# Scan: mix and scores as 64x64 quarters, keys of odd channel tiles with halves exchanged

## The reference, cut to what matters

```python
def step(state, inp):
    x_t, b_t, c_t, dt_t = inp
    decay = jnp.exp(dt_t * a)[..., None, None]
    b_bar = dt_t[..., None] * b_t
    state = decay * state + b_bar[..., None] * x_t[:, :, None, :]
    y_t = jnp.einsum('bhn,bhnp->bhp', c_t, state)
    return (state, y_t)
```

## Time and profile before

| | |
|---|---|
| median of 3 runs | 1251.53 us (1251.30 to 1253.37) |
| profiled execution | 1251.51 us, span 1249.4 us |
| PE busy | 1233.5 us, 99% of the span |
| PE weight load | 1029.7 us, 82% |
| DVE busy | 923.6 us, 74% |
| POOL busy | 775.0 us, 62% |
| ACT busy | 612.0 us, 49% |
| granted clock of PE | 1.000 |

### The profile page before, as it was taken

One profiled execution on the slowest core, in us unless ns is written; L12 is line 12 of the kernel. 1 busy time (PEld: TensorE's weight loads), 2 busy tenths in 40 slices (PEclk: granted clock), 3 DMA queues, 4 the chain that ended last, 5 costly groups with the idle time before them and its releaser, 6 DMA issues.

```text
span 1249.4 us, 28240 instructions
## 1 busy us (share of the span) xinstructions
PE 1233.5 (99%) x11183; PEld 1029.7 (82%) x11185; DVE 923.6 (74%) x1868; ACT 612.0 (49%) x1276; POOL 775.0 (62%) x660
## 2 busy tenths in 40 slices
PE   8999999999999999999999999999999999999999
PEld 4666678888888888888888887789989999899998
DVE  7999877777675677677766657897777766776676
ACT  6999974444434344433433334444344332554453
POOL 4889845345454476666766656566666754566773
PEclk9999999999999999999999999999999999999999
DMA  9799759353454444435434445574455544799995
GB/s 293 258 338 351 292 202 211 135 170 128 141 173 141 166 134 133 156 147 178 136 121 166 148 144 175 191 176 89 92 114 95 96 92 105 230 322 332 334 320 176
DMA packets 122211, 231.18 MB, mean 185 GB/s; under 512 B 19168, under 2 KB 85984, under 8 KB 113760
## 3 DMA queue, kind: packets, MB, share of 16 engines
q1 hardware_dynamic: 108928, 212.08, 50.5%
q0 software_dynamic: 12288, 17.05, 8.0%
q10 hardware_dynamic: 864, 0.24, 0.1%
HBM read 147.81 MB, written 81.53 MB: 184 GB/s over the span
## 4 chain that ended last, share of the span: by engine, by line
PE 76%; DVE 8%; ACT 4%; POOL 4%; DMA 3%; issue 3%; SPq 1%; POOLq 0%; another core or an unknown queue 0%; ACTq 0%; DVEq 0%
PE ps L1273 22%; PE ps L1613 9%; PE ps L1870 8%; PE ps L2104 7%; PE ps L2083 7%; PE ps L1398 4%; PE ps L1328 3%; PE ps L1410 2%; PE ps L1361 2%; PE ps L1378 2%; PE ps L1344 2%; DMA y_dram<-yb 2%; PE ps L693 2%; PE ps L641 1%; ACT decay L1240 1%
## 5 line engine op out<-in xcount | busy, mean ns | idle before, releaser
L1240 ACT ACTIVATE decay<-tap,ncum 128x128 f32<-128x128 f32 x344 | 105.4, 389 | 150.5 <-POOL tap L1153 150.5
L1798 POOL DMA_INDIRECT ffn_dram<-ob,idx x64 | 110.3, 1724 | 81.6 <-DVE ob L1717 67.8
L1071 DVE TENSOR_TENSOR yb<-ps,yb 128x256 f32<-128x256 f32 x128 | 48.4, 420 | 146.0 <-PE ps L1410 141.3
L1832 ACT ACTIVATE mid<-ps,b_up 128x512 f32<-128x512 f32 x96 | 65.9, 689 | 156.0 <-PE ps L1613 130.4
L1182 POOL TENSOR_SCALAR yb<-x,dcol 128x512 f32<-128x512 f32 x64 | 48.9, 764 | 129.9 <-DMA y_dram<-yb 95.3
L1159 POOL TENSOR_TENSOR x_lo<-x,x_hi 128x512 fp32r<-128x512 f32 x56 | 73.6, 1314 | 80.5 <-ACT x_hi L1226 80.4
L1170 POOL TENSOR_TENSOR c_dec<-cT,ecum_row 128x512 f32<-128x512 f32 x64 | 89.2, 1394 | 35.9 <-PE ps L1410 26.3
L1273 PE MATMUL ps<-x_hi,w_hi_b 128*128 128x512 f32 x240 | 99.6, 415 | 0.6 <-ACT bT L1230 0.6
L1273 PE MATMUL ps<-x_hi,w_hi_c 128*128 128x512 f32 x240 | 99.4, 414 | 0.0
L1959 POOL TENSOR_SCALAR yc<-yc,gn_scale,gn_shift 128x512 f32<-128x512 f32 x56 | 76.7, 1381 | 32.4 <-DMA yc<-y_dram 32.4
L1273 PE MATMUL ps<-x_lo,w_hi_b 128*128 128x512 f32 x240 | 94.4, 393 | 0.0
(11 more groups left out here) (313 smaller groups left out, 3948.0 us busy)
## 6 DMA issues: line engine op xcount, KB each, us to landing
tap<-cum_dram SPq DMA_DIRECT2D x43, 512.0 KB
x_dram<-x SPq DMA_DIRECT2D x16, 1024.0 KB, 5.7
x<-x_dram SPq DMA_DIRECT2D x16, 1024.0 KB, 5.6
ecum_row<-ecum_dram SPq DMA_DIRECT2D x128, 128.0 KB
y_dram<-yb SPq DMA_DIRECT2D x16, 1024.0 KB, 7.4
yc<-y_dram SPq DMA_DIRECT2D x16, 1024.0 KB, 6.8
cum_row<-cum_dram SPq DMA_DIRECT2D x21, 512.0 KB
rows_dram<-xn SPq DMA_DIRECT2D x16, 512.0 KB, 3.3
```

The source lines that it names most:

```text
L1240: n = nc.scalar.activation(decay[g % 2][:, h, :], cum_row[g % NR][:, h, :], ACT.Exp, bias=t.ncum[:, g, h:h + 1])
L1798: pool.indirect_dma_start(out=t.ffn_dram, out_offset=bass.IndirectOffsetOnAxis(ap=t.idx[:, e, h * HC + c:h * HC + c + 1], axis=0), in_=ob[ ...
```

## The change

The masked quarter is left out. The key halves are called p (where they lie: partitions 0 to 63 or 64 to 127). For queries of the first half only early keys count. So that both row halves of the PE array get equal work, the two key halves of odd channel tiles are exchanged: `key_half(q, p)` is p for even q and 1 - p for odd. Partition p of an odd tile then holds the other half of the chunk's tokens, in x2 (loaded in five DMAs, `load_turned`), in bT (ACT's copy), in dt, ncum, gap and the mask. Where the key half is the late one, scores and mix have 64 columns instead of 128. The mix contracts 64 keys at a time and sums the halves in two banks, ps_y[0] and ps_y[1], which are now full, so DVE adds two operations of 512 columns into yb. The update goes into ps_r (upper half), ahead of the mix in every chunk, and is started anew each time. The lists no longer accumulate in ps_r: each chunk's sum is added by DVE into SBUF (`add_lists`), and the two zero matmuls go. The store of y to memory is issued a chunk earlier (c == 0).

```diff
+def load_turned(sp, dst, src, loaded):
+    sp.dma_start(dst[:, 0:4:2, :], src[:, 0:4:2, :]).then_inc(loaded, 16)
+    for m in (1, 3):
+        for j in range(2):
+            sp.dma_start(halves(dst[:, m, :])[:, :, 1 - j, :], halves(src[:, m, :])[:, :, j, :]).then_inc(loaded, 16)
@@ front, DVE: gap, ncum and dt each as three operations
+            def do_turned(op, *aps, name):
+                parts = [a.rearrange("p t (a k i) -> p k t a i", a=2, k=2) for a in aps]
+                do(op(*(a[:, 0] for a in parts)))
+                for r in range(2):
+                    own, other = (slice(j * s.HD, (j + 1) * s.HD) for j in (r, 1 - r))
+                    do(op(parts[0][own, 1], *(a[other, 1] for a in parts[1:])), name if r else None)
@@ DVE, chunk(g)
+        def add_lists(k, g):
+            dve.wait_ge(tile_used, k + 1)
+            dve.wait_ge(s_mm, updates(g + 1))
+            flat = lists[:, :, :, :, :].rearrange("p a b k l -> p (a b k l)")
...
+                v.tensor_tensor(flat, ps_list, flat, ALU.add).then_inc(lists_read, 1)
-            for a in range(2):
-                own_half = yb[b % 2][:, 2 * a:2 * a + 2, cols]
-                n = v.tensor_tensor(own_half, ps_y[a][:, 0:HW].rearrange("p (m n) -> p m n", m=MT // 2), own_half,
-                                    ALU.add)
-            n.then_inc(y_ready, 1)
+            if LIST0 <= g < LIST1:
+                add_lists(g - LIST0, g)
+            y_out, (y_0, y_1) = yb[b % 2][:, :, cols], [a[:, :].rearrange("p (m n) -> p m n", m=MT) for a in ps_y]
+            v.tensor_tensor(y_out, y_0, y_out, ALU.add).then_inc(y_step, 1)
             update(g)
+            dve.wait_ge(y_step, g + 1 + g // SPAN + 1)
+            v.tensor_tensor(y_out, y_1, y_out, ALU.add).then_inc(y_ready, 1)
@@ SP
-            if c == 1 and b:
+            if c == 0 and b:
@@ POOL, causal(g)
+            nc.gpsimd.affine_select(out=even, in_=even, compare_op=ALU.is_ge, fill=-1e30, base=0,
+                                    pattern=[[0, H // 2], [1, P]], channel_multiplier=-1)
+            nc.gpsimd.affine_select(out=odd[:, :, 0:HD], in_=odd[:, :, 0:HD], compare_op=ALU.is_ge, fill=-1e30, base=HD,
+                                    pattern=[[0, H // 2], [1, HD]], channel_multiplier=-1).then_inc(row_ready, 1)
+            pool.wait_ge(row_ready, 2 * g + 1)
+            nc.gpsimd.affine_select(out=odd[0:HD], in_=odd[0:HD], compare_op=ALU.is_ge, fill=-1e30, base=-HD,
+                                    pattern=[[0, H // 2], [1, P]], channel_multiplier=-1).then_inc(row_ready, 1)
@@ PE, scores(g)
+                for p, a in ((0, 0), (1, 1), (1, 0), (0, 1)):
+                    n = (m + 2 * p) % MT
+                    r, j = slice(a * HD, (a + 1) * HD), key_half(n // 2, p)
+                    keys = bT[b % 2][r, n, c * P + p * HD:c * P + (p + 1) * HD]
+                    mm = pe.matmul(ps_g[a][p * HD:(p + 1) * HD, n * P + j * HD:(n + 1) * P],
+                                   keys, cT[b % 2][r, n, c * P + j * HD:(c + 1) * P],
@@ PE, update(g), ahead of the mix
+            pe.wait_ge(x_dt_ready, g + 1)
+            pe.wait_ge(b_w_ready, updates(g) + 1)
+            if g < ROUNDS:
+                pe.wait_ge(bit_step, 4 * g + 2)
+            elif SLOTS < g < SLOTS + CH:
+                pe.wait_ge(sel_step, steps[("limits", "offset", "slot_i")[g - SLOTS - 1]])
+            if g == LAST + 1:
+                pe.wait_ge(x.xg_lo_ready, 2 * s.KT)
+            elif g == LAST + 2:
+                pe.wait_ge(x.mid_ready, 2)
@@ PE, the mix
+            for r, tiles in enumerate(((0, 1), (2, 3), (1, 0), (3, 2))):
+                for i, p in ((0, 0), (1, 1), (1, 0), (0, 1)):
+                    q, rows = tiles[p], slice(p * HD, (p + 1) * HD)
+                    h, j = 2 * q + i, key_half(q, p)
+                    mm = pe.matmul(ps_y[p][i * HD:(i + 1) * HD, q * P + j * HD:(q + 1) * P],
+                                   x_dt[rows, h * HD:(h + 1) * HD], mix[rows, h, j * HD:P],
+                                   start=(r == 0), stop=(r >= 2), skip_group_check=True)
```

More of the change, by code:

```diff
@@ L535, in _ @@
                 tile_copy(n)
-            act.wait_ge(x2_back[1], 16)
+            act.wait_ge(x2_back[1], TURNED)
             for m in range(MT):
-                nc.scalar.activation(t.x_hi[1][:, m, :], x2[1][:, m, :], ACT.Copy).then_inc(x1_hi, 1)
+                nc.scalar.activation(*t.turned(t.x_hi[1][:, m, :], x2[1][:, m, :], m % 2), ACT.Copy).then_inc(x1_hi, 1)
             act.wait_ge(vec, steps["cum"])
@@ L908, in updates, with listed, added, key_half @@
         return g - g // SPAN
+    t.state_ready, t.updates = state_ready, updates
     def loads(b, n):
         return 16 * (b // n + 1)
+    def listed(g):
+        return min(max(g - LIST0, 0), LIST1 - LIST0)
+    def added(g):
+        bank = ps_pc if g == LAST + 1 else ps_pb if g == LAST + 2 else ps_r
+        return bank[:, LISTS:LISTS + MT * HD]
+    def key_half(q, p):
+        return p ^ (q % 2)
     @block.vector
@@ L1025, in update, with clear_y @@
                 dve.wait_ge(s_mm, updates(g) + 1)
-                v.tensor_tensor(state[:, :, :], added, state[:, :, :], ALU.add).then_inc(state_ready, 1)
+                v.tensor_tensor(state[:, :, :], new, state[:, :, :], ALU.add).then_inc(state_ready, 1)
+        def clear_y(g):
+            if g == 0:
+                dve.wait_ge(t.tile_out, 2 * MT)
+                for p in range(2):
+                    n = v.memset(ps_y[p][:, :], 0.0)
+            else:
+                dve.wait_ge(y_ready, g)
+                for p in range(2):
+                    q = 1 + p
+                    n = v.memset(ps_y[p][:, q * P:q * P + HD], 0.0)
+            n.then_inc(y_step, 1)
         def chunk(g):
@@ L1379, in _ @@
                 mm.then_inc(b_turned, 1)
+            until(pe, state_ready, updates(g))
             if g < ROUNDS:
                 total(g)
+            elif SLOTS <= g < SLOTS + CH:
+                slots(c)
             if b + 1 < NB:
@@ L1385, in _ @@
                 x.up(pe, 0, 0, range(2 * c - 2, 2 * c - 1))
+            until(pe, lists_read, listed(g))
             if LIST0 <= g < LIST1:
                 list_tiles(g - LIST0)
+            if not last:
+                update(g)
             until(pe, y_ready, g)
-            until(pe, state_ready, updates(g))
+            pe.wait_ge(y_step, g // SPAN * (SPAN + 1) + 1)
             pe.wait_ge(x_dt_ready, g + 1)
             pe.wait_ge(mix_ready, 2 * g + 2)
-            if first:
-                own_parts(g)
-            for a in range(2):
-                for m in range(MT):
-                    h = a * MT + m
-                    mm = pe.matmul(y_of(a, m), x_dt[:, h * HD:(h + 1) * HD], mix[:, h, :],
-                                   start=(m < 2 and not (first and a == 0)), stop=(first and m >= 2),
-                                   skip_group_check=True)
-            if first:
-                mm.then_inc(y_mm, 1)
-            elif not last:
-                own_parts(g)
+            mm = own_parts(g)
             if not first:
                 pe.wait_ge(c_dec_ready, g + 1)
-                for m in range(0, MT, 2):
-                    for i, a in ((0, 0), (1, 1), (1, 0), (0, 1)):
-                        r = slice(a * HD, (a + 1) * HD)
-                        mm = pe.matmul(y_of(a, m + i), state[r, m + i, :], c_dec[r, m + i, :], start=False,
-                                       stop=(m == MT - 2), skip_group_check=True)
-                mm.then_inc(y_mm, 1)
+                mm = state_parts(g)
+            mm.then_inc(y_mm, 1)
             if g + 1 < NT:
@@ L1609, in up @@
                 pe.wait_ge(mid_ready, n - 2)
+            if n in (0, 2, 4):
+                pe.wait_ge(t.state_ready, t.updates(s.NT - 3 + n // 2))
             i = 0
```

147 lines of the change are left out of this document (77 added, 70 removed).

## The result

The changed kernel takes 1246.01 us (median of 5, 1243.34 to 1251.24), the kernel before 1251.53; the ratio is 0.9944, 95% interval 0.9920 to 0.9967. So it is faster, but by 5.5 us where 16.0 were forecast, and 1246.0 against 1235.5.

The account below looks back on a forecast made before the run. PE was taken to bound the kernel, with DVE next. Terms: -26.0 (scores, mix) - 0.5 (lists' matmuls) + 6.5 (list stage) + 3.5 (end) + 0.5 (front) = -16.0, from 1251.53 to 1235.5 us; range 1229 to 1243.

Parts of the forecast that it names:

- Scores and mix, -26.0: Scores and mix on PE: masked quarters at 64 columns save 0.204 us each, 0.408 a chunk, 26.0 over 64 chunks.
- the 0.5 us of the lists' two matmuls: Lists on PE: dropping the 512-column matmuls that open and close the bank saves 0.5 us with their switches.
- The rival with 0.100 us a four: Scores and mix: four tiles don't go faster with fewer columns; fours gain only 4.6 us, about 1255 us; chance 0.07.
- The remark that the switches of form stay at one: PE array: the number of form switches stays; 128x64 to 64x64 moves from between update and state to update and mix.
- List stage, +6.5: 32 list chunks: DVE's longer loop makes PE wait for b_w; 5.8 us over 22 chunks, taken as 6.5 with POOL.
- one deadline, b_w before the update: List chunks: DVE's y-to-y loop through b_w takes 12.02 - i (i: wait before y); a chunk loses max(0, 2.74 - i).
- The mean of DVE's collisions: List stage: SBUF-only DVE operations stretch beside POOL; the second one-hot operation averages 1.12 us where b_w takes 0.68.
- End of the scan, +3.5: Chunks 61 to 63: update waits for token remainders (y 1.8 us later), DVE's additions and unsaved scores; sum 3.5 us.
- Costed at nothing: Stages without lists: b_w and y fit DVE's room; updates' waits in search and slot chunks are met before PE arrives.
- Hidden, as said: POOL's longer mask, x in five DMAs, halved mask-row loads and SP's extra DMAs: no cost in the scan.
- my bound of 12 us from the mean packet: Loads of x: each small piece at the queue's mean per packet, 93 ns, says 12 us more; hidden either way.
- The front, +0.5: Before chunk 0: split gap and ncum operations and later landing of x cost 0 to 4 us, taken as 0.5.

## Why the prediction was wrong, step by step

**Scores and mix, -26.0: right.** Full against short columns differ by 0.206 us for the scores and 0.206 for the mix (0.984 to 0.778, 0.924 to 0.718, medians of the list chunks), where the prediction had 0.204 each; PE's busy time fell by 25.2 (the 0.5 us of the lists' two matmuls can't be told apart in it). The rival with 0.100 us a four is out. The remark that the switches of form stay at one was right too, but I didn't see what hung on it: it holds only because the update went ahead of the mix, and the old order would have cost some 12 us, more than the change brings.

**List stage, +6.5: the step that failed.** It cost 9.4 us, and none of it by the way that the prediction took. I set DVE's loop against one deadline, b_w before the update. In the stage that wait doesn't occur once. DVE has an earlier one: x_dt before the turns of the keys, 5.2 us after the mix begins (587.66 and 592.85), with 0.77 us to spare. All that the change adds to DVE (0.34 for the lists, the second bank of y) stands ahead of it. Six chunks lost 5.9 us by it (five 1.02 to 1.04, one 0.74); the version with the addition moved gave back 4.1. The longer additions alone don't explain it, though: with the mix over 128 keys, where y is emptied in short ones, x_dt cost 6.0 us. What counts as much is where the decay starts among POOL's operations: with the list sum moved from ahead of it (and the second addition too) no decay was shut out for long. What POOL's mask in three operations has to do with it isn't shown. The mean of DVE's collisions was also wrong as a measure: its groups show

```profile
L1085 DVE TENSOR_TENSOR state<-state,dec 128x256 f32<-128x256 f32 x31 | 27.8, 896 | 0.0
L1050 DVE TENSOR_TENSOR spare<-chosen,cst 128x512 bf16<-128x512 f32 x30 | 22.7, 758 | 0.0
...
L1050 DVE TENSOR_TENSOR spare<-gateT,cst 128x512 bf16<-128x512 f32 x30 | 20.5, 684 | 0.0
...
L1064 DVE TENSOR_TENSOR lists<-ps,lists 128x256 f32<-128x256 f32 x31 | 13.2, 425 | 77.8 <-PE ps L1454 75.1 <-PE ps L1443 2.7
```

The one-hot operation `spare<-gateT` that took 1115 ns takes 684, so DVE collides less in sum, which is why b_w is early. But the decay went from 742 to 896, ahead of x_dt: a chunk has a collision of 1.7 us or none. The rest, 3.7 us in two chunks (periods of 11.21 and 10.76 for 9.29, with 0.3 in the next), is the stalls of PE without a releaser, which no part of the prediction had.

**End of the scan, +3.5: right in mechanism and nearly in size.** Chunks 60 to 63 lost 4.7. The update of chunk 61 waits 1.67 us for xg_lo (forecast 1.8):

```profile
775.49 1.29 DVE L1658 TENSOR_TENSOR xg_lo<-ps,xg_hi 128x512 fp32r<-128x512 f32 x2 [0.58 <-ACT xg_hi L1653]
...
776.93 0.69 PE L1432 MATMUL ps<-x_dt,b_w 128*64 128x64 f32 x16 [1.67 <-DVE xg_lo L1658]
```

**Costed at nothing, and not nothing.** Chunks 0 to 2 lost 1.7 us, of which the update of chunk 0 waiting for the kept list is 1.1; I had looked only at b_w there. Chunks 15 to 24 lost 1.5, again such stalls (0.5 and 0.7 us idle at 353 and 363 us). The 0.9 us of chunks 56 to 60 I didn't follow up.

**Hidden, as said.** The loads of x: the version with one DMA was no faster, so my bound of 12 us from the mean packet was far off. The mask on POOL takes 1.80 us (0.65, 0.46, 0.69) where 1.38 were forecast, and POOL isn't late; but its third operation is one that the decay runs into. The front, +0.5: chunk 0 began 1.2 us earlier in this execution, 0.5 in the second; no cost.

**What stays open.** The time of the changed kernel varies by 7.9 us over five executions; its profiled one is the fastest. The median is 2.7 us above it, against none before the change. Part of it goes with the clock: the five slowest of the thirteen executions of the changed kernel (1246.99 to 1251.24 us) have a mean granted clock of 0.997 and the other eight 0.998 to 1.000, while all 33 of the kernel before in the experiments have 1.000. My estimate from these figures: 0.003 of 1241 us, up to 3.7 us, is what the lower clock costs such an execution. Eight of the twelve profiles show where, falls to 0.50 between 762 and 793 us, among the waits at the end of the scan; the profiled execution of the changed kernel, its fastest, has none. So the profile that the table splits is a little better than the median. What decides whether the clock falls there wasn't tested, nor whether the stalls differ between executions. A mask on POOL that keeps clear of the decay wasn't tried.

## What to carry to other kernels

Before work is added to an engine off the path, list every deadline that it has in a period, not the one with the most waiting behind it: the room to the first of them counts, against the worst collision of one period and not the mean. When matmuls are cut into smaller tiles, group them so that the form of the array changes as seldom as before. And when PE's time falls while its instruction count rises, look in the new trace for idle time without a releaser, and for a granted clock that falls behind it.

## What the runs showed of the hardware

Four 64-column passes in four 64x64 tiles go at 0.058 us a four (starts at 521.32, 521.38, 521.44), and four of 128 columns at 0.109: eight short fours save 0.41 us. Two further changes of the tile form cost PE 0.09 and 0.11 us. A DVE operation with two SBUF inputs was shut out by two POOL operations in a row (2.10 us for 0.42) when it started 0.06 us behind the first. PE stood still without a releaser for 0.4 to 2.2 us, in the middle of 32 short matmuls too, and resumed 2.2 to 2.85 us after a load on the instruction queue had begun. Behind two of these stalls, of 1.98 and 2.24 us, the granted clock was at its lower level (586.0 to 589.4 and 534.0 to 537.4 us) and matmuls of 512 columns went at 0.43 us instead of 0.23. And in one execution it was at that level from 193.5 to 200.3 us, during and behind 64 matmul rows of one column that began at 191.8.
